# Moving one difference and one row sum of a paired secular solve from VectorE to ScalarE

## What is computed

```
deg = jnp.sum(A, axis=-1)
Lap = deg[..., :, None] * jnp.eye(n, dtype=A.dtype) - A
Lap_norm = d_isqrt[..., :, None] * Lap * d_isqrt[..., None, :]
_, U = jnp.linalg.eigh(Lap_norm)
agg = jnp.einsum('bmn,bmd->bnd', U, features)
h = jax.nn.relu(jnp.einsum('bnd,hd->bnh', agg, W0) + b0)
out = jnp.einsum('bnh,oh->bno', h, W1) + b1
ret = jnp.einsum('bnm,bmo->bno', U, out)
```

## Time and profile before

| what | value |
|---|---|
| median of 3 runs | 6887.09 us (6878.48 to 6890.2) |
| profiled execution, its own time | 6893.13 us |
| its span, first to last instruction | 6891.4 us |
| VectorE busy | 5295.9 us, 77% |
| TensorE busy | 2513.4 us, 36% |
| ScalarE busy | 1080.2 us, 16% |
| GpSimd busy | 1129.2 us, 16% |
| TensorE's mean granted clock | 0.651 of full speed |

### The profile page before, as it was taken

The page is one execution under the profiler, slowest core; times in us unless marked ns, Lnnn a source line. Parts: engine busy times, 40 slices in busy tenths (PEclk is TensorE's granted clock), DMA queues, the critical chain, the costliest instruction groups (busy, mean ns, idle before and its releaser), DMA issues.

```text
span 6891.4 us, 60101 instructions
## 1 busy us (share of the span) xinstructions
PE 2513.4 (36%) x16082; PEld 1640.2 (24%) x16082; DVE 5295.9 (77%) x19524; ACT 1080.2 (16%) x3167; POOL 1129.2 (16%) x1482
## 2 busy tenths in 40 slices
PE   0444444444255371917171154010384000100476
PEld 0112112222132231414051143010373000100354
DVE  5565666566699999999788977999798999999400
ACT  0000000000122313122130021000131000000255
POOL 0000000000054444445422121010331000100000
PEclk9666666655567585857585577555697555555688
DMA  3000000000100000000102003100002000100110
GB/s 84 12 14 25 15 14 15 16 18 21 30 7 7 7 13 7 13 7 0 13 14 43 0 7 69 24 0 0 6 13 93 24 0 0 61 0 0 37 49 13
DMA packets 143486, 136.22 MB, mean 20 GB/s; under 512 B 36541, under 2 KB 128330, under 8 KB 136650
## 3 DMA queue, kind: packets, MB, share of 16 engines
q1 hardware_dynamic: 143178, 132.78, 7.0%
HBM read 106.24 MB, written 26.41 MB: 19 GB/s over the span
## 4 chain that ended last, share of the span: by engine, by line
DVE 70%; PE 17%; DMA 5%; issue 3%; ACT 3%; POOL 1%; SPq 1%; DVEq 0%; ACTq 0%; POOLq 0%; PEldq 0%
PE psum L1799 6%; DVE big_b L1014 3%; DVE big_a L1024 2%; DVE big_a L1022 2%; DVE ms L1025 2%; PE psum L1817 2%; DVE ms L1058 2%; DVE big_b L1057 2%; DVE big_b L615 2%; DVE gvec L345 2%; DVE big_b L628 2%; DVE big_b L1018 2%; DVE big_a L374 1%; DVE big_b L1012 1%; DVE big_b L618 1%
## 5 line engine op out<-in xcount | busy, mean ns | idle before, releaser
L1799 PE MATMUL psum<-big_a 128*32 128x508 f32 (+59 forms) x4032 | 439.9, 607 | 39.5 <-ACT big_a L1762 39.5
L1940 PE MATMUL psum<-plane,big_b 128*128 128x128 f32 x192 | 37.1, 374 | 933.1 <-DVEq L1138 916.7
L1257 DVE RECIPROCAL f_ln<-f_ln 128x16 f32<-128x16 f32 x20 | 5.1, 253 | 428.4 <-ACT f_ln L1366 426.9
L1622 POOL TENSOR_TENSOR big_a<-big_a,plane 128x2048 f32<-128x2048 f32 x28 | 183.1, 6540 | 759.4 <-ACT big_a L1586 625.3
L1930 PE MATMUL psum<-big_b 128*128 128x128 f32 x384 | 68.4, 361 | 652.5 <-ACT big_b L1878 652.5
L1452 PE MATMUL psum<-plane,big_a 128*128 128x128 f32 x192 | 50.2, 430 | 670.7 <-ACT big_a L1373 649.2
L682 POOL TENSOR_TENSOR big_b<-big_b 128x128 f32<-128x128 f32 x615 | 286.5, 466 | 48.2
L1847 ACT ACTIVATE ms<-ms 128x64 f32<-128x64 f32 (+1 forms) x36 | 8.7, 243 | 1797.2 <-DVE ms L1078 1645.5
L677 POOL TENSOR_TENSOR big_b<-big_b 128x512 f32<-128x512 f32 (+1 forms) x164 | 168.4, 1027 | 738.0 <-DVEq L507 728.3
L1961 POOL MEMSET big_b<- 128x2304 f32 x1 | 2.0, 2023 | 1733.3 <-DVEq L396 1733.3
L374 DVE TENSOR_TENSOR big_a<-big_a,psum 128x504 f32<-128x504 f32 (+16 forms) x272 | 98.1, 422 | 238.0 <-PE psum L1817 238.0
(11 more groups left out here) (664 smaller groups left out, 10623.1 us busy)
## 6 DMA issues: line engine op xcount, KB each, us to landing
big_a<-rows_dram SPq DMA_DIRECT2D x4, 4096.0 KB, 12.1
vt<-pairs_dram SPq DMA_DIRECT2D x504, 32.0 KB
big_a<-rows_dram SPq DMA_DIRECT2D x4, 2048.0 KB, 17.7
big_a<-rows_dram SPq DMA_DIRECT2D x2, 3072.0 KB, 14.4
big_b<-rows_dram SPq DMA_DIRECT2D x2, 3072.0 KB, 21.3
big_a<-x SPq DMA_DIRECT2D x16, 256.0 KB, 3.4
big_a<-adjT SPq DMA_DIRECT2D x16, 256.0 KB, 3.7
x_dram<-big_a SPq DMA_DIRECT2D x16, 256.0 KB, 2.4
```

Source lines behind the costliest of these rows:

```text
L1622: ins = p.tensor_tensor(level, q_gram, over(pl[f"upper{s}"], FG, 1), ALU.mult).then_inc(S("level_ready"), 1)
L1799: ins = t.matmul(psum[i * SPAN:i * SPAN + MW, 0, 0:4 * wide], v_masked[:, i, q * MW:(q + 1) * MW], anode[:, g:g + 4, k + 1:N + 2 * u], sta ...
```

## The change

With two solves in a pair, the differences of the second solve are formed by ScalarE (`diff - eta` as `Identity` with the bias `eta_neg`, one instruction per piece, into `row_tiles[:, 1]`), and the slopes of the first solve are summed by ScalarE (`Copy` with an accumulated output, one instruction per piece, in place on `row_tiles[:, 2]`). VectorE forms `eta_neg` at the start of a turn. Four semaphores tie them: `guess_ready`, `apart_ready`, `slope_ready`, `slope_summed`. As the loop now writes tiles 1 and 2 of the rows, SP waits for `solved` before it fetches the four kinds of the next pair. The unpaired level (blocks of 32) keeps its instructions.

```
-                def invert():
+                def invert(of=mt):
-                    lo, hi = mt[:, :, 0:hb], mt[:, :, hb:]
+                    lo, hi = of[:, :, 0:hb], of[:, :, hb:]
...
                 with v.Fori(0, ROOT_ITERS) as it:
                     lp.rewind()
-                    for h in both:
-                        sums(h)
-                        lp(v.tensor_tensor(mr, mt, mr, ALU.mult))
-                        n_s = lp.go(v.tensor_reduce(mine(dfe, h), mr, X, ALU.add))
-                        if h < halves - 1:
-                            lp.after(n_s)
+                    nth = i * ROOT_ITERS + it + (PAIRED[lev] * ROOT_ITERS - ROOT_ITERS + 1)
+                    if halves == 2:
+                        v.tensor_scalar(mine(eta_neg, 1), mine(eta, 1), -1.0, None, ALU.mult).then_inc(S("guess_ready"), 1)
+                        sums(0)
+                        v.wait_ge(S("slope_summed"), nth)
+                        v.tensor_tensor(slope, mt, mr, ALU.mult).then_inc(S("slope_ready"), 1)
+                        v.wait_ge(S("slope_ready"), nth)
+                        v.wait_ge(S("apart_ready"), nth)
+                        invert(apart)
+                        lp(v.tensor_tensor(mt, wx[1], mr, ALU.mult))
+                        lp.go(v.tensor_reduce(mine(fe, 1), mt, X, ALU.add))
+                    else:
+                        sums(0)
+                    lp(v.tensor_tensor(mr, mt, mr, ALU.mult))
+                    lp.go(v.tensor_reduce(mine(dfe, halves - 1), mr, X, ALU.add))
+                    if halves == 2:
+                        v.wait_ge(S("slope_summed"), nth + 1)
```

ScalarE, in the place where it only served the square roots:

```
-                        with a.Fori(0, r1 - r0) as it:
+                        with a.Fori(0, min(r1, ROOT_ITERS) - r0) as it:
+                            if PAIR[lev] == 2:
+                                nth = i * ROOT_ITERS + it + (PAIRED[lev] * ROOT_ITERS - ROOT_ITERS + 1 + r0)
+                                a.wait_ge(S("guess_ready"), nth)
+                                for g in range(GS[lev]):
+                                    at = GS[lev] + g
+                                    ins = a.activation(tile_g(row_tiles[:, 1, :], g), tile_g(second_tiles[:, 0, :], g), ACT.Identity,
+                                                       bias=ms[:, 27, at:at + 1])
+                                ins.then_inc(S("apart_ready"), 1)
+                                a.wait_ge(S("slope_ready"), nth)
+                                for g in range(GS[lev]):
+                                    src = tile_g(row_tiles[:, 2, :], g)
+                                    ins = a.activation(src, src, ACT.Copy, accum_out=ms[:, 10, g:g + 1])
+                                ins.then_inc(S("slope_summed"), 1)
                             root(i * (ROOT_ITERS + 1) + it + (base + 1 + r0), ms[:, 15, 0:width])
+                    root(i * (ROOT_ITERS + 1) + (base + 1 + ROOT_ITERS), ms[:, 15, 0:width])
```

SP:

```
                     sy.wait_ge(S("deflate_spread"), i * PAIR[lev] + (SOLVES[lev] + 1))
+                    sy.wait_ge(S("solved"), i + (PAIRED[lev] + 1))
                     rows_from(row_tiles[:, 0:4], slice(0, 4), 0, "scan_rows_in")
-                    sy.wait_ge(S("solved"), i + (PAIRED[lev] + 1))
                     rows_from(row_tiles[:, 4:7], slice(4, 7), 0, "pole_rows_in")
```

More of the change, by code:

```diff
@@ L963, in v_level_merge @@
             (gap, last, wsum, wn, right, org, wc, sgm, eta, fe, dfe, y0, dy, cc, aa, qq, num, den, t0, t1, on,
-             own_w, own_d, offv, le, wd, qx) = (q(i) for i in range(27))
+             own_w, own_d, offv, le, wd, qx, eta_neg) = (q(i) for i in range(28))
+            apart, slope = cmp_(row_tiles[:, 1, :]), cmp_(row_tiles[:, 2, :])
             diag_c, super_c = pl[f"diag{blk}"][:, 0:blk], pl[f"super{blk}"][:, 0:blk]
@@ L1836, in _ @@
             v.sem_inc(S("solved"), 1)
+            v.sem_inc(S("slope_summed"), 1)
             for lev in range(len(LEVELS)):
@@ L1884, in _ @@
                         r1 = r0 + 2 if u < subs - 1 else ROOT_ITERS + 1
-                        with a.Fori(0, r1 - r0) as it:
+                        with a.Fori(0, min(r1, ROOT_ITERS) - r0) as it:
+                            if PAIR[lev] == 2:
+                                nth = i * ROOT_ITERS + it + (PAIRED[lev] * ROOT_ITERS - ROOT_ITERS + 1 + r0)
+                                tile_g = lambda t, g: t[:, g * blk:(g + 1) * blk]
+                                a.wait_ge(S("guess_ready"), nth)
[9 more added lines that the diff above has]
+                                ins.then_inc(S("slope_summed"), 1)
                             root(i * (ROOT_ITERS + 1) + it + (base + 1 + r0), ms[:, 15, 0:width])
+                    root(i * (ROOT_ITERS + 1) + (base + 1 + ROOT_ITERS), ms[:, 15, 0:width])
                     for u in range(subs):
```

## The result

| what | before | after |
|---|---|---|
| median of 4 runs each | 6885.28 us (6878.48 to 6890.2) | 6792.45 us (6791.93 to 6796.04) |
| profiled execution, its span | 6891.4 us | 6790.5 us |
| VectorE busy | 5295.9 us | 5192.1 us |
| ScalarE busy | 1080.2 us | 1356.7 us |

The ratio of the times is 0.9865, 95% interval 0.9851 to 0.9879: 1.35% faster, by 92.8 us. The forecast was 6792.6 us, 94.5 us less than the 6887.1 us that it went by. The profiled execution of after lies on the median of its runs (6792.29 us).

A forecast was written before the change was run, and what follows sets the result against it. VectorE's own chain was taken to bound the paired loop's 24 turns. Savings of 105.6 us less 11.1 us for the moved wait gave -94.5 us, from 6887.1 to 6792.6 us; range 6780 to 6821, with table loads 6780 to 6825.

The forecast's parts named there:

- The chain: Paired loop: turns are VectorE's own chain; 50.49 us at 64 becomes 46.1, 48.99 us at 128 becomes 44.6.
- The fourth rival: Paired loop: the passes removed were not on the chain; time within 0.2% of before or some us above; chance 2%.
- What leaves VectorE: Each turn: second solve's difference 2.33 us and first solve's slope sum 2.32 us; 4.65 us, 111.6 us over 24 turns.
- What VectorE gets: Each turn: negated guess 0.10 us, two waits before `invert(apart)` 0.15 us; 0.25 us taken, bounds 0.10 to 0.60 us.
- the hold: Third turn: GpSimd holds VectorE ahead of the edited instructions, L1018 taking 5.55 us instead of 1.23; stays unchanged.
- What ScalarE gets: Each turn: differences at 0.39 us and slope sums at 0.30 us a piece, hidden under 18.5 and 18.4 us.
- the tight case: Third turn at 64: copies of `w` and `y` come first; differences end at 16.6 us, 1.9 us before wanted.
- The slow rival: Each turn: VectorE waits for ScalarE; no gain at 0.94 us slope pieces; chance 3% slower than before, 5% partly late.
- the threshold of 0.57 us: Slope sums at 64: pieces under 0.57 us cost nothing; above it each 0.1 us costs 3.2 us per turn.
- Table loads: Rival: a 1.283 us load before the square root in each of 24 turns, 31 us, time 6823; chance 4%.
- The moved wait: Start of the second pair at 128: 30.10 us from SP's issue to first subtraction, not 18.98; 11.1 us more, once.
- The rival in which `deflation(0)` waits for all three transfers: Start of the second pair at 128: transfers share the queue, 24.8 us in place of 11.1, time 6806; chance 6%.

The follow-up runs named there:

- each half: The changed kernel with only the differences on ScalarE: 6839.7 us, ratio 0.9933; with only the slope sums there: 6841.18 us, ratio 0.9931.
- the kernel with the value sum: The changed kernel with the first solve's sum of values `fe` also on ScalarE: 6737.35 us; with idle slots and early fetch as well: 6724.01 us.

## Why the prediction was right

- **The chain.** Turns of 45.95 and 44.43 us against 46.1 and 44.6 forecast. All three loops together give 109.9 us where 105.6 were expected, and each half gives its own part: the turns were VectorE's own chain. The fourth rival (passes not on the chain) is out.
- **What leaves VectorE** was right: 24 instructions fewer (L1022 and L1058 -48, the negated guess +24; the page counts 19524 and 19500).
- **What VectorE gets** was the term that was mis-sized: 0.25 us a turn taken, 4.65 - 4.54 = 0.11 measured, next to the lower bound of the step. The price of an exposed wait, 0.11 us, was carried over to the two waits before `invert(apart)` with "cannot hide". The first of them only took the place of `lp`'s wait, and the second showed no price: the `invert` instruction starts 2.32 us after the slope product. (0.25 - 0.11) x 24 = 3.4 us of the 4.3 by which the loops beat the forecast; 0.6 more come from the three long turns at 64, which save 0.20 us more than the others, where the prediction had the hold "stays as it is".
- **What ScalarE gets.** It was covered, but the price was too high at the narrow size, as the step said it might be: 0.24 us for a difference at 64 and 0.30 at 128 in place of 0.39 for both, 0.24 us for a sum at 64 in place of 0.30. The piece with a bias and a scale in the earlier trace rows cost more, 0.39 against 0.30 us at the same 128 columns. So the tight case (third turn) had 14.8 us to spare and not 1.9: of the 12.9 between, 4.8 us are the price, 0.6 that the pieces could start sooner (4494.85, 3.6 us into the turn, not 4.1), and 7.5 VectorE's own delay while GpSimd works (3.98 and 5.40 us for passes of 0.69 and 1.22), which the prediction named but did not count.
- **The slow rival** needed pieces of 0.94 us. Three times the measured price is 0.72 us a sum, and that made VectorE wait 39 us at 64 and not at all at 128, as the threshold of 0.57 us says: (0.72 - 0.57) x 32 x 8 = 38 us, measured 38.8.
- **Table loads.** None came, and the rival's price was wrong too: 31 us for 24 loads in the chain, and nothing measured for 48, all of which were run in time that ScalarE had to spare.
- **The moved wait** was right: 30.21 us from issue to first subtraction against 30.10, 11.2 to 11.3 us in the stage against 11.1. The rival in which `deflation(0)` waits for all three transfers is out, since it began 12.1 us after the issue.
- **The median** came out at 6792.45 against 6792.6, closer than the terms are: the loops gave 4.3 us more than forecast, and the untouched stages moved by several us either way between executions (-8.8 and +5.9 in the two profiles). The median before also came out 1.8 us lower with a fourth run. The agreement to 0.2 us is luck; to some 5 us it is the sum.

## What to carry to other kernels

Where one engine is the chain and another sits idle beside it, a pass is worth its full time even if the idle engine needs three times as long for it; what decides is the time between the moment its input is there and the moment the result is wanted, measured turn by turn, and the turn in which the idle engine has other work first. After such a move measure what is left of that cover: here it was 10.7 us in each place, enough for one more sum. And ask where the new results are written: a tile that a transfer fills early brings a wait with it, and two idle slots took 7.5 of its 11.3 us back in one kernel and all of it in another.

## What was not expected of the hardware

- Narrow pieces on ScalarE overlap. Differences of 64 columns last 334 ns and cost 0.24 us each in a row of them; sums last 239 ns with 186 ns for the accumulator's read and also start 0.24 us apart.
- A satisfied wait on a register's value, behind the wait for the end of the pass before, cost nothing between the slope product and `invert` (2.32 us from start to start at 64, 2.31 at 128), where the earlier trace rows showed 0.11 us for one, and the two products of the kernel with the value sum, with such a pair of waits between them, 2.41 - 2.32 = 0.09 us (below). What tells the places apart was not tried.

```profile
5458.66 2.29 DVE L1061 TENSOR_TENSOR big_a<-big_a,big_b 128x2048 f32<-128x2048 f32 x1
5461.07 2.29 DVE L1064 TENSOR_TENSOR big_a<-big_a,big_b 128x2048 f32<-128x2048 f32 x1
```

- A table load was run ahead of the wait of the activation that needs it (load at 4424.95, activation at 4438.45).
- Stages that no edit touches differ by more than 10 us from one execution to the next (the start by 12.8 us, 4382.38 to 4395.14), which is more than the moved wait costs here: 11 us could be told only by the stage and by many runs.
